# Summing two scan units by four products of 64 rows and 64 columns, and without folding quads by DMA

## The chip, the core and the metric

The kernel runs on one NeuronCore of a Trainium2 chip. A time is the device time of one execution in microseconds (us); the figure for a kernel is the median of its runs. The core has a matrix engine (TensorE, PE in the profile, with its weight loads as PEld), VectorE (DVE), ScalarE (ACT), GpSimd (POOL), SyncE (SP), which here only starts transfers, and DMA queues.

## The reference, cut to what matters

A batch of 8 sequences of 512 tokens and 256 features goes through four layers: a linear attention (layer 0), two selective state-space layers (1 and 2) and another linear attention (layer 3). The two state-space layers fill nearly the whole time, and the change is in them. Each has 512 channels and 16 states per channel:

```python
def step(h, inp):
    dt_t, B_t, C_t, u_t = inp
    dA = jnp.exp(dt_t[:, :, None] * A)
    h = h * dA + (dt_t * u_t)[:, :, None] * B_t[:, None, :]
    y = jnp.einsum('bdn,bn->bd', h, C_t)      # the sum over the 16 states
    return (h, y)
...
y = jnp.transpose(ys, (1, 0, 2)) + u * D_param
y = y * jax.nn.silu(z)
return jnp.einsum('bsd,ed->bse', y, out_proj_w)
```

## The kernel before, in words

**Tiling.** A scan is one state-space layer of one sequence: 16 in all (`SCANS`). The 512 channels are 4 chunks of 128 partitions, the 512 tokens lie in the free dimension. The chunks are taken in two halves of 2 chunks. A **unit** is one state n of one chunk: a tile of 128 partitions x 512 tokens of float32. Unit g of a half is state n = g // 2 and chunk c2 = g % 2; two units that share a state are a **pair**. So a half has 32 units (16 pairs), a scan 64, the kernel 1024 units or 512 pairs.

**A unit's way.** ScalarE makes the decay `exp(dt * A)` (L1028 in a PSUM bank, L1044 in SBUF). The input dt*u*B is made for a pair at once, by GpSimd (L756, kind BESIDE, 192 pairs) or by VectorE (L1318, kind SPREAD, 320 pairs, from a B row that ScalarE copied into a bank, L1036). VectorE runs the recurrence over the tokens, unit by unit (`scan`, L1325 and L1328). GpSimd multiplies the pair by its row of C (`weight`, L765). TensorE sums over the states (`sum_up`, L1648): the identity times the state tile, added up in one of two PSUM banks, `y_banks[c2]`, one for each chunk. The first product of a bank is `skip` (L1638), the diagonal matrix of D times u. After the last sum VectorE multiplies the bank by silu(z) (`gate`, L1340), and `m_gate` tells TensorE that the bank may be used again. The state tiles stand in a ring of 20 (`STATES`); `state_free` waits until a slot has been summed.

**Folding.** Four units in a row are a quad, 8 quads a half. `FOLDS = ((0, 1), (3, 4))` names two quads a half that are not summed by TensorE but added onto the next one by a DMA that accumulates in SBUF (`fold`, L769, started by GpSimd). TensorE then sums 24 of the 32 units of a half; the units of quads 1 and 4 come late (`FOLDED_LAG` 14 units after their scan, the others `SUM_LAG` 5), and wait for the DMA (`m_fold`).

**Order.** Every engine walks the same clock of units (`run_batches`): at unit g it issues its own part of unit g, and chains of other work (attention of other sequences, the preparation of the next scan, the output of the last one) are laid between the units by hand-written tables of ticks (`ATT_STAGES`, `PREP_STAGES`, `POST_STAGES`, ...; `HALF_STEPS` sets how far ahead ScalarE and GpSimd issue). `sum_ticks` says at which unit which sum is issued (`SUMS_AT`), and `GATE_TICKS` at which unit VectorE gates a bank. Each engine executes its own list strictly in order, so a waiting instruction holds all behind it. On TensorE the sums stand between the products of attention (L1416 to L1494), of the preparation (L1516 to L1555) and of the output (L1602, L1610).

**Numbers to keep in mind.** A float32 product of TensorE is shown by the profile as two records of MATMUL, each with its own LDWEIGHTS. 32 halves x 24 sums are 768 products (1536 records at L1648), and 64 skips are 128 records at L1638.

Of the kernel before, what the change touches and what calls it, by code (L numbers as in the profile page):

```python
# [5 lines left out]
P = 128  # L6
B, T, D = 8, 512, 256
TT, DC = T // P, D // P
DI, CH, N = 512, 4, 16
# [8 lines left out]
HALVES = 2  # L18
# [4 lines left out]
PAIRS = B // 2  # L23
SLOTS = 4

SUM_LAG = 5
BANKS, DECAYS, STATES, ROWS = 3, 7, 20, 4
QUAD = 4
FOLDS = ((0, 1), (3, 4))
FOLD_LAG = 2  # L30
# [216 lines left out]
def sum_ticks():  # L247

    at = {}
    for g in range(ALL_UNITS):  # L250
        if not fold_from(g):
            at.setdefault(g + (FOLDED_LAG if fold_into(g) else SUM_LAG), []).append(g)
    return at
# [3 lines left out]
SUM_ORDER = [g for tick in sorted(SUMS_AT) for g in SUMS_AT[tick]]  # L257
SUM_COUNT = {g: n for n, g in enumerate(SUM_ORDER, 1)}
BANK_SUMS = {}
for unit_ in SUM_ORDER:  # L260
    BANK_SUMS.setdefault((unit_ // HALF_UNITS, unit_ % HC), []).append(unit_)
GATE_TICKS = tuple(max(t for t, units in SUMS_AT.items() for k in units if k < HALF_UNITS and k % HC == c2) + 1 - HALF_UNITS
                   for c2 in range(HC))

# [156 lines left out]
def bass_cond_seq(nc, x, out, mask_cols, keep_cols, mask_rows0, mask_rows3, order, const_pack, att_packs, ssm_packs,  # L421
# [4 lines left out]
    with ctx:  # L426
# [634 lines left out]
        def _(dve):  # L1061
# [268 lines left out]

            def gate(si, half, c2):

                layer, s = scan_of(si)
                c = half * HC + c2
                if c == 0:
                    taken(dve, prep_fill(si, "z2"))
                    taken(dve, prep_fill(si, "z3"))
                dve.wait_ge(m_sum, SUM_COUNT[BANK_SUMS[si * HALVES + half, c2][-1]])
                taken(dve, prep_fill(si, f"z{c}"))
                dve.tensor_tensor(u[s][:, c, :], y_banks[c2][:], zh[s][:, c, :], ALU.mult).then_inc(m_gate, 1)  # L1340

            def unit(g, part):
                if part == 0:
                    for first in (g, g + 1):
                        if is_unit(first) and first % HC == 0 and kind_of(first) == SPREAD and PRODUCT_LEAD[first // HC] == first - g:
                            inject(first)
                    return
                if is_unit(g):
                    scan(g)
                for c2, tick in enumerate(GATE_TICKS):  # L1350
                    if g % HALF_UNITS == tick and is_unit(g - HALF_UNITS):
                        si, half, *_ = split(g - HALF_UNITS)
                        gate(si, half, c2)

# [4 lines left out]
        def _(pe):  # L1359
# [268 lines left out]

            def skip(si, half, c2):
                layer, s = scan_of(si)  # L1630
                c = half * HC + c2
                if c < HC:
                    pe.wait_ge(s_gate_nat, 2)
                    pe.wait_ge(s_mod[3], 1)
                    pe.wait_ge(s_skip, 2)
                past(pe, m_gate, si * CH + c - HC + 1)
                pe.wait_ge(p_u, si * CH + c + 1)
                pe.matmul(y_banks[c2][:], skip_diag[layer][:, c, :], u[s][:, c, :], start=True, stop=False)  # L1638

            def sum_up(g):  # L1640
                si, half, n, c2, c = split(g)
                in_bank = BANK_SUMS[g // HALF_UNITS, c2]
                if g == in_bank[0]:
                    skip(si, half, c2)
                pe.wait_ge(m_prod, g // HC + 1)
                for n in fold_into(g):
                    pe.wait_ge(m_fold[n], 16 * (g // HALF_UNITS) + 16)
                pe.matmul(y_banks[c2][:], ident, state[:, g % STATES], start=False, stop=(g == in_bank[-1])).then_inc(m_sum, 1)  # L1648

# [91 lines left out]
```

## Time and profile before

| | |
|---|---|
| median of 3 runs | 2156.11 us (2149.99 to 2160.99) |
| span of the profiled execution | 2153.9 us |
| VectorE busy | 1935.2 us, 90% |
| TensorE busy | 1887.8 us, 88% |
| GpSimd busy | 1821.9 us, 85% |
| ScalarE busy | 1719.8 us, 80% |
| mean granted TensorE clock | 0.968 of full speed |

The median lies 2.2 us over the span of the one profiled execution. Busy shares are means over the span. The first 200 us (set-up, two attentions of sequences 0 and 1, the first preparation) and the last 110 us (output and a lone attention) look different from the 1800 us between, in which the scans run back to back.

### The profile page before, as it was taken

The numbers are of one execution on the slowest core, as the hardware profiler recorded it, in microseconds if no ns is written. First come the engines' busy times: TensorE is split into PE (matmuls) and PEld (weight loads), VectorE is DVE, ScalarE is ACT, GpSimd is POOL, SyncE is SP. The second block draws the span as 40 slices with busy tenths as digits, with TensorE's granted clock in tenths as the row PEclk, the third lists the DMA queues.
The fourth block names the chain that finished last, engine by engine and source line by source line (L and its number), as shares of the span: only waits on it lengthen the run. The fifth ranks groups of instructions, "written<-read, shape, count | busy, mean of one in ns | idle before, by whom it ended". The sixth has DMA issues, their size and how long they took to land. (4 is left out here: it accounts for less than half of the span.)

```text
span 2153.9 us, 22717 instructions
## 1 busy us (share of the span) xinstructions
PE 1887.8 (88%) x5980; PEld 975.5 (45%) x5980; DVE 1935.2 (90%) x2022; ACT 1719.8 (80%) x3125; POOL 1821.9 (85%) x906
## 2 busy tenths in 40 slices
PE   8968789899888989899898989899899988778798
PEld 7533334445354544445454443535445443324356
DVE  5479999999999999999999998999999999899963
ACT  2387788888889888898989888888989987677652
POOL 0088998989898998989899997989989898989950
PEclk9889989999999999999999999999999999899999
DMA  6056665656466575646656675555556666555630
GB/s 247 1 170 174 176 195 150 196 168 185 138 178 176 165 207 166 196 146 180 173 160 187 176 209 155 167 176 164 171 165 195 173 181 179 174 166 176 192 93 20
DMA packets 170543, 358.77 MB, mean 167 GB/s; under 512 B 19544, under 2 KB 27952, under 8 KB 161712
## 3 DMA queue, kind: packets, MB, share of 16 engines
q1 hardware_dynamic: 151958, 279.32, 39.8%
q0 software_dynamic: 9216, 67.11, 15.3%
q10 hardware_dynamic: 9242, 10.89, 1.5%
q8 instruction: 49, 0.80, 0.1%
q14 instruction: 78, 0.64, 0.1%
HBM read 284.85 MB, written 5.29 MB: 135 GB/s over the span
## 5 line engine op out<-in xcount | busy, mean ns | idle before, releaser
L765 POOL TENSOR_TENSOR state<-state,c_rows 128x1024 f32<-128x1024 f32 x512 | 1214.9, 2410 | 139.2 <-DVE state L1328 95.8
L1648 PE MATMUL bank<-state,const_sb 128*128 128x512 f32 x1536 | 775.3, 620 | 111.2 <-POOL state L765 63.7
L1328 DVE TENSOR_TENSOR_SCAN state<-decay,mix_banks 128x512 f32<-128x512 f32 x640 | 753.2, 1207 | 31.5 <-ACT decay L1044 14.5
L1325 DVE TENSOR_TENSOR_SCAN state<-mix_banks,state 128x512 f32<-128x512 f32 x384 | 450.4, 1204 | 30.5 <-ACT mix_banks L1028 19.7
L1648 PEld LDWEIGHTS bank<-state,const_sb 128*128 128x128 f32 x1536 | 282.2, 196 | 423.9 <-issue 252.3
L756 POOL TENSOR_TENSOR state<-kept,b_rows 128x1024 f32<-128x1024 f32 x192 | 469.1, 2443 | 3.4 <-DMA b_rows<-flat_rows 1.7
L1044 ACT ACTIVATE decay<-kept,ssm_pack 128x512 f32<-128x512 f32 x640 | 435.3, 711 | 1.0
L1318 DVE TENSOR_TENSOR mix_banks<-kept,mix_banks 128x1024 f32<-128x1024 f32 x320 | 392.8, 1227 | 28.9 <-ACT mix_banks L1036 19.6
L1028 ACT ACTIVATE mix_banks<-kept,ssm_pack 128x512 f32<-128x512 f32 x384 | 259.5, 683 | 115.7 <-DVE state L1328 101.2
L1544 PE MATMUL bank<-kept,ssm_pack 128*128 128x512 f32 x512 | 244.2, 613 | 25.9 <-DVE kept L1277 8.4
L1036 ACT ACTIVATE mix_banks<-b_rows 128x512 f32<-128x512 f32 x320 | 187.8, 591 | 51.2 <-DVE state L1328 27.6
L1435 PE MATMUL bank<-att_pack,xnT 128*128 128x256 f32 x704 | 202.1, 405 | 0.0
L1544 PEld LDWEIGHTS bank<-kept,ssm_pack 128*128 128x128 f32 x512 | 96.4, 195 | 146.2 <-issue 105.6
L1602 PE MATMUL bank<-kept 128*128 128x256 f32 x512 | 130.0, 396 | 16.2 <-DVE kept L1291 16.2
L708 POOL TENSOR_TENSOR att_rstd<-att_var_eps,neg_half 128x4 f32<-128x4 f32 x32 | 35.4, 1105 | 120.1 <-DVE att_minus L1165 112.3
L1435 PEld LDWEIGHTS bank<-att_pack,xnT 128*128 128x128 f32 x704 | 119.2, 189 | 37.6 <-issue 8.1
L1277 DVE SCALAR_TENSOR_TENSOR kept<-bank,ssm_pack,kept 128x511 f32<-128x511 f32 (+2 forms) x192 | 128.7, 737 | 7.4 <-ACT kept L974 7.1
L1602 PEld LDWEIGHTS bank<-kept 128*128 128x128 f32 x512 | 99.9, 201 | 47.5 <-issue 35.9
L728 POOL TENSOR_TENSOR kept<-kept 128x1024 f32<-128x1024 f32 x32 | 77.5, 2421 | 48.3 <-ACT kept L942 48.3
L1044 ACT ACT_TABLE_LOAD x82 | 105.2, 1283 | 1.5
L1422 PE MATMUL bank<-xnT,att_pack 128*128 128x512 f32 x120 | 60.1, 624 | 21.7 <-ACT xnT L875 16.0
L1416 PE MATMUL bank<-const_sb,xn 128*128 128x128 f32 x352 | 56.7, 285 | 25.0 <-ACT xnT L929 8.8
(198 smaller groups left out, 2208.7 us busy)
## 6 DMA issues: line engine op xcount, KB each, us to landing
b_rows<-flat_rows SPq DMA_DIRECT2D x512, 256.0 KB, 3.9
c_rows<-flat_rows SPq DMA_DIRECT2D x512, 256.0 KB, 3.6
state<-state POOLq DMA_DIRECT2D x64, 1024.0 KB, 9.7
out<-x_res ACTq DMA_DIRECT2D x8, 512.0 KB, 7.4
ssm_pack<-ssm_pack SPq DMA_DIRECT2D x2, 2035.0 KB, 13.2
x_next<-x ACTq DMA_DIRECT2D x6, 512.0 KB, 7.2
state<-ada_w SPq DMA_DIRECT2D x1, 1536.0 KB, 12.3
kept<-ada_w SPq DMA_DIRECT2D x1, 1536.0 KB, 15.1
```

What stands on the lines that cost most here:

```text
L756: pool.tensor_tensor(pair_states(g), dtu[:, c:c + HC], by_pair(b_rows[:, row % ROWS]), ALU.mult).then_inc(m_inject[BESIDE], 1)
L765: pool.tensor_tensor(st, st, by_pair(c_rows[:, row % ROWS]), ALU.mult).then_inc(m_prod, 1)
L1028: act.activation(mix_banks[BANK_OF[g]], dt[:, c, :], ACT.Exp, scale=neg_a[scan_of(si)[0]][:, c * N + n:c * N + n + 1]).then_inc(m_decay[BE ...
L1036: act.activation(mix_banks[ROW_BANK[g // HC]], b_rows[:, row % ROWS], ACT.Copy).then_inc(m_brow, 1)
L1044: act.activation(decay[:, nth(g) % DECAYS, :], dt[:, c, :], ACT.Exp, scale=neg_a[scan_of(si)[0]][:, c * N + n:c * N + n + 1]).then_inc(m_d ...
L1318: dve.tensor_tensor(both, dtu[:, c:c + HC, :], by_pair(mix_banks[row]), ALU.mult).then_inc(m_inject[SPREAD], 1)
L1325: ins = dve.tensor_tensor_scan(st, mixed, st, 0.0, ALU.mult, ALU.add)
L1328: ins = dve.tensor_tensor_scan(st, decay[:, nth(g) % DECAYS], mixed, 0.0, ALU.mult, ALU.add)
L1435: ins = pe.matmul(dst, lhs[:, c, t * P:(t + 1) * P], weights[:, c, :], start=(c == 0 and bias is None), stop=(c == DC - 1))
L1544: ins = pe.matmul(dst[:], w_in[:, c, (at + e) * P:(at + e + 1) * P], xnT_[:, c, :], start=(c == 0), stop=(c == DC - 1))
L1602: ins = pe.matmul(dst[:, (t % 2) * D:(t % 2 + 1) * D], lhs[:, c, t * P:(t + 1) * P], weights[:, c, :], start=(c == 0), stop=(c == CH - 1))
L1648: pe.matmul(y_banks[c2][:], ident, state[:, g % STATES], start=False, stop=(g == in_bank[-1])).then_inc(m_sum, 1)
```

## The change

The two PSUM banks no longer stand for the two chunks of a half but for the two row halves of a chunk (`ROW_HALVES`, partitions 0 to 63 and 64 to 127). Bank k takes the rows of half k: chunk 0 in its partitions 0 to 63, chunk 1 in 64 to 127. A pair is summed by four products with 64 rows and 64 columns of the identity, one for each combination of row half and chunk; each uses one quarter of the array, and the four use different quarters. Only the last of the four raises `m_sum`, and counts are now per pair. The skip product is cut in the same way. `FOLDS` is empty: no fold transfers, no `m_fold`, and all 16 pairs of a half are summed, each 5 units after its second unit (`SUM_LAG`). `gate` runs for both banks at one unit (`GATE_TICK`), after the last pair of the half, and the first skip of a half waits until both banks of the half before are gated. So that the gated result has its channels in the new order, the columns of `w_in` that make z and the rows of `w_out` are permuted on the host (`by_half`).

```diff
+ROW_HALVES = (slice(0, P // 2), slice(P // 2, P))
-FOLDS = ((0, 1), (3, 4))
+FOLDS = ()
...
-    for g in range(ALL_UNITS):
+    for g in range(0, ALL_UNITS, HC):
         if not fold_from(g):
-            at.setdefault(g + (FOLDED_LAG if fold_into(g) else SUM_LAG), []).append(g)
+            at.setdefault(g + 1 + (FOLDED_LAG if fold_into(g) else SUM_LAG), []).append(g)
...
-                dve.wait_ge(m_sum, SUM_COUNT[BANK_SUMS[si * HALVES + half, c2][-1]])
+                dve.wait_ge(m_sum, SUM_COUNT[HALF_SUMS[si * HALVES + half][-1]])
                 taken(dve, prep_fill(si, f"z{c}"))
-                dve.tensor_tensor(u[s][:, c, :], y_banks[c2][:], zh[s][:, c, :], ALU.mult).then_inc(m_gate, 1)
+                dve.tensor_tensor(u[s][:, c, :], y_banks[k][:], zh[s][:, c, :], ALU.mult).then_inc(m_gate, 1)
...
-                past(pe, m_gate, si * CH + c - HC + 1)
-                pe.wait_ge(p_u, si * CH + c + 1)
-                pe.matmul(y_banks[c2][:], skip_diag[layer][:, c, :], u[s][:, c, :], start=True, stop=False)
+                past(pe, m_gate, si * CH + half * HC)
+                pe.wait_ge(p_u, si * CH + half * HC + HC)
+                for k, rows in enumerate(ROW_HALVES):
+                    for c2, to in enumerate(ROW_HALVES):
+                        c = half * HC + c2
+                        pe.matmul(y_banks[k][to, :], skip_diag[layer][rows, c, rows], u[s][rows, c, :], start=True, stop=False)
...
-                pe.matmul(y_banks[c2][:], ident, state[:, g % STATES], start=False, stop=(g == in_bank[-1])).then_inc(m_sum, 1)
+                for k, rows in enumerate(ROW_HALVES):
+                    for c2, to in enumerate(ROW_HALVES):
+                        ins = pe.matmul(y_banks[k][to, :], ident[rows, rows], state[rows, (g + c2) % STATES],
+                                        start=False, stop=(g == in_half[-1]))
+                ins.then_inc(m_sum, 1)
...
+    by_half = np.arange(DI).reshape(HALVES, HC, 2, P // 2).transpose(0, 2, 1, 3).reshape(DI)
...
+        w_in = np.concatenate([w_in[:, :DI], w_in[:, DI:][:, by_half]], axis=1)
+        w_out = w_out[by_half]
```

What it moves shows in the order of the instructions. The skip line is L1638 before and L1640 now, the sum line L1648 before and L1652 now; one row of the order is one product (not one record), `x4` four in a row. First TensorE, where the second half of the third scan (the first of layer 2) begins: L1533 and L1544 prepare the next scan, L1416, L1422 and L1424 are attention. Before:

```order
242 L1533 MATMUL bank<-permute,kept 128x512 x2
243 L1648 MATMUL bank<-state,const_sb 128x512
244 L1533 MATMUL bank<-permute,kept 128x512 x2
245 L1648 MATMUL bank<-state,const_sb 128x512
246 L1533 MATMUL bank<-permute,kept 128x512
247 L1416 MATMUL bank<-const_sb,xn 128x128 x4
248 L1544 MATMUL bank<-kept,ssm_pack 128x512 x4
249 L1416 MATMUL bank<-const_sb,xn 128x128 x4
250 L1422 MATMUL bank<-xnT,att_pack 128x512 x2
251 L1424 MATMUL bank<-right_rows,bias_rows 128x512
252 L1544 MATMUL bank<-kept,ssm_pack 128x512 x4
253 L1638 MATMUL bank<-kept,skip_diag 128x512
```

And TensorE at the same place now:

```order
241 L1652 MATMUL bank<-state,const_sb 64x512 x4
242 L1533 MATMUL bank<-permute,kept 128x512
243 L1416 MATMUL bank<-const_sb,xn 128x128 x4
244 L1640 MATMUL bank<-kept,skip_diag 64x512 x4
245 L1652 MATMUL bank<-state,const_sb 64x512 x4
246 L1544 MATMUL bank<-kept,ssm_pack 128x512 x4
247 L1652 MATMUL bank<-state,const_sb 64x512 x4
248 L1416 MATMUL bank<-const_sb,xn 128x128 x4
249 L1652 MATMUL bank<-state,const_sb 64x512 x4
250 L1422 MATMUL bank<-xnT,att_pack 128x512 x2
251 L1424 MATMUL bank<-right_rows,bias_rows 128x512
252 L1652 MATMUL bank<-state,const_sb 64x512 x4
```

The skip has moved to the front of the half, and a group of four small products stands between the other work at each pair. Over the whole program there are 544 such groups (512 sums, 32 skips) in 425 places, at 347 of them a single group. Products that use another part of the array than the one before them follow each other 1250 times now and 540 times before.

GpSimd, in the same half, about the second of its two folds; L756 and L765 are the input and the weighting of a pair, L728 part of the preparation. Before:

```order
133 L765 TENSOR_TENSOR state<-state,c_rows 128x1024 x2
134 L728 TENSOR_TENSOR kept<-kept 128x1024
135 L765 TENSOR_TENSOR state<-state,c_rows 128x1024
136 L769 DMA state<-state 128x2048
137 L756 TENSOR_TENSOR state<-kept,b_rows 128x1024
138 L765 TENSOR_TENSOR state<-state,c_rows 128x1024 x3
```

The same place now; only the DMA of the quad has gone:

```order
116 L765 TENSOR_TENSOR state<-state,c_rows 128x1024 x2
117 L728 TENSOR_TENSOR kept<-kept 128x1024
118 L765 TENSOR_TENSOR state<-state,c_rows 128x1024
119 L756 TENSOR_TENSOR state<-kept,b_rows 128x1024
120 L765 TENSOR_TENSOR state<-state,c_rows 128x1024 x3
```

VectorE, at the end of a half, as a piece of the difference (the scan is listed under another name here, and L1340 is the gate):

```order
-L1328 SCALAR_TENSOR_TENSOR state<-decay,mix_banks 128x512 x2
-L1340 TENSOR_TENSOR kept<-bank,kept 128x512
-L1328 SCALAR_TENSOR_TENSOR state<-decay,mix_banks 128x512
-L1340 TENSOR_TENSOR kept<-bank,kept 128x512
+L1328 SCALAR_TENSOR_TENSOR state<-decay,mix_banks 128x512 x3
+L1340 TENSOR_TENSOR kept<-bank,kept 128x512 x2
```

The first of the two gates has moved back by one scan, next to the second.

## Rows read from the trace of the kernel before

**Rows 1.** The page's part 1: busy us (share of the span) xinstructions of each engine.

```profile
PE 1887.8 (88%) x5980; PEld 975.5 (45%) x5980; DVE 1935.2 (90%) x2022; ACT 1719.8 (80%) x3125; POOL 1821.9 (85%) x906
```

**Rows 2.** Busy us of each engine by stretch, then granted clock, DMA share, GB/s.

```profile
core 0: us, PE busy (x) PEld busy (x) DVE busy (x) ACT busy (x) POOL busy (x), PEclk, DMA share, GB/s
0.00:100.00 100.00, 89.44 (x466) 64.89 (x467) 49.80 (x142) 31.80 (x55) 7.02 (x18) 0.90 0.37 134
100.00:200.00 100.00, 71.56 (x202) 33.39 (x202) 81.80 (x80) 81.69 (x147) 80.83 (x40) 0.90 0.53 159
...
600.00:800.00 200.00, 178.73 (x568) 91.64 (x567) 193.96 (x190) 178.47 (x345) 190.74 (x94) 0.99 0.64 187
800.00:1000.00 200.00, 183.28 (x561) 89.35 (x560) 189.70 (x192) 176.73 (x305) 179.80 (x88) 1.00 0.56 165
...
2050.00:2154.00 104.00, 93.24 (x478) 65.04 (x476) 48.49 (x77) 36.09 (x72) 29.80 (x18) 0.99 0.17 50
```

**Rows 3.** Waits of VectorE, 200 to 1900 us: us in total, times, longest.

```profile
DVE mix_banks L1318 <- ACT mix_banks L1036: 18.1, 18, 2.8
DVE state L1328 <- ACT decay L1044: 13.4, 7, 4.7
DVE qstat L1217 <- PE bank L1435: 7.5, 6, 1.3
DVE state L1325 <- ACT mix_banks L1028: 5.5, 9, 1.0
DVE state L1325 <- POOL state L756: 4.7, 9, 1.0
DVE kept L1277 <- ACT kept L974: 4.2, 4, 2.4
DVE x_res L1298 <- PE bank L1602: 4.1, 1, 4.1
```

**Rows 4.** Waits of TensorE in the same stretch, the longest two.

```profile
PE bank L1648 <- POOL state L765: 45.7, 49, 4.0
PE bank L1648 <- DMA state<-state: 43.3, 27, 5.1
```

**Rows 5.** Groups by line and shape: busy us, mean ns, then idle before.

```profile
L1648 PE MATMUL bank<-state,const_sb 128*128 128x512 f32 x1536 | 775.3, 620 | 111.2 <-POOL state L765 63.7 <-DMA state<-state 47.0
L1638 PE MATMUL bank<-kept,skip_diag 128*128 128x512 f32 x128 | 67.8, 612 | 0.0
L1516 PE MATMUL bank<-x_dbl,ssm_pack 64*128 64x512 f32 x128 | 63.5, 616 | 3.1 <-ACT x_dbl L983 3.1
L769 POOL DMA_DIRECT2D state<-state x64 | 55.8, 872 | 0.0
```

**Rows 6.** TensorE's timeline: start us, us, instructions; full-array products in a row.

```profile
1003.32 1.02 PE L1638 MATMUL bank<-kept,skip_diag 128*128 128x512 f32 x2
1004.17 1.02 PE L1648 MATMUL bank<-state,const_sb 128*128 128x512 f32 x2
1005.03 0.59 PE L1602 MATMUL bank<-kept 128*128 128x256 f32 x2
1005.46 1.02 PE L1638 MATMUL bank<-kept,skip_diag 128*128 128x512 f32 x2
```

**Rows 7.** TensorE's timeline where 64-row products (L1516) stand between full ones.

```profile
359.67 1.45 PE L1648 MATMUL bank<-state,const_sb 128*128 128x512 f32 x3
361.05 1.98 PE L1516 MATMUL bank<-x_dbl,ssm_pack 64*128 64x512 f32 x4
362.96 2.41 PE L1648 MATMUL bank<-state,const_sb 128*128 128x512 f32 x5
```

**Rows 8.** The chain that ended last, near its end: start us, us, what.

```profile
1986.45 10.69 DMA state<-state
```

**Rows 9.** Who waited for the gate (L1340), and for whom it waited: us, times.

```profile
  PE bank L1648: 6.3, 6
who waited for it (us, times):
  PEld bank L1602: 17.4, 3
```

More of the change, by code:

```diff
@@ L257 @@
 SUM_ORDER = [g for tick in sorted(SUMS_AT) for g in SUMS_AT[tick]]
[L258 to L263, printed above, removed]
+SUM_COUNT = {g + k: n for n, g in enumerate(SUM_ORDER, 1) for k in range(HC)}
+HALF_SUMS = {}
+for pair_ in SUM_ORDER:
+    HALF_SUMS.setdefault(pair_ // HALF_UNITS, []).append(pair_)
+GATE_TICK = max(t for t, pairs in SUMS_AT.items() for k in pairs if k < HALF_UNITS) + 1 - HALF_UNITS
 def prep_fill(pi, what):
@@ L1329, in scan, with gate @@
                 ins.then_inc(m_scan, 1)
-            def gate(si, half, c2):
+            def gate(si, half, k):
                 layer, s = scan_of(si)
-                c = half * HC + c2
+                c = half * HC + k
                 if c == 0:
@@ L1349, in unit @@
                     scan(g)
[L1350 to L1353, printed above, removed]
+                if g % HALF_UNITS == GATE_TICK and is_unit(g - HALF_UNITS):
+                    si, half, *_ = split(g - HALF_UNITS)
+                    for k in range(HC):
+                        gate(si, half, k)
             run_batches(setup, attention, before, tail, after, unit)
@@ L1627, in after, with skip @@
                 yield from w.to("end")
-            def skip(si, half, c2):
+            def skip(si, half):
                 layer, s = scan_of(si)
-                c = half * HC + c2
-                if c < HC:
+                if half == 0:
                     pe.wait_ge(s_gate_nat, 2)
@@ L1635, in skip @@
                     pe.wait_ge(s_skip, 2)
-                past(pe, m_gate, si * CH + c - HC + 1)
-                pe.wait_ge(p_u, si * CH + c + 1)
-                pe.matmul(y_banks[c2][:], skip_diag[layer][:, c, :], u[s][:, c, :], start=True, stop=False)
+                past(pe, m_gate, si * CH + half * HC)
[4 more added lines that the diff above has]
+                        pe.matmul(y_banks[k][to, :], skip_diag[layer][rows, c, rows], u[s][rows, c, :], start=True, stop=False)
             def sum_up(g):
[L1641 to L1644, printed above, removed]
+                si, half, *_ = split(g)
+                in_half = HALF_SUMS[g // HALF_UNITS]
+                if g == in_half[0]:
+                    skip(si, half)
                 pe.wait_ge(m_prod, g // HC + 1)
```

## The prediction, made before the kernel ran

> **What bounds the kernel now.** I read the page's first part and the busy time by stretch first [rows 1, 2]. VectorE has the largest share, 1935.2 of 2153.9 us, and between 600 and 1000 us, where the scans run back to back, it is busy 194.0 and 189.7 of 200 us. TensorE has 178.7 and 183.3 there and GpSimd 190.7 and 179.8. VectorE's idle time lies at the two ends: 50.2 and 18.2 us in the first two stretches, 55.5 us in the last. Between 200 and 1900 us its seven longest waits add up to 57.5 us [rows 3]: 41.2 for ScalarE, 11.6 for TensorE, 4.7 for GpSimd. So the kernel is bound by VectorE, with GpSimd and TensorE close behind. TensorE's own waits are for its inputs: 45.7 us for GpSimd's weighting and 43.3 us for the fold transfer [rows 4]. It is not the bound, but it has only 266 us to spare over the whole span. Whoever adds more than that makes it the bound.
>
> **What a product costs.** The sums are 1536 records in 775.3 us, the skips 128 in 67.8 us [rows 5]: together 843.1 us. All else on TensorE is 1887.8 - 843.1 = 1044.7 us. In a row of full products the next one starts 0.85 and 0.86 us later [rows 6], so a record takes 0.43 us of the array, and each shown record has a tail of about 0.17 us behind it (1.02 for two records). A product on half the rows is no shorter: L1516 works on 64 rows and shows 616 ns where the sums have 620 and the skips 612 [rows 5]. So each of the four small products takes the two records of 0.43 us of a full one, and the change can win on TensorE only if products in different quarters of the array run at the same time. No row of before shows two products in separate parts of the array side by side; this is the unknown on which all hangs.
>
> **A change of the part in use.** Between 359.67 and 365.37 us stand 3 full records, 4 of 64 rows and 5 full ones [rows 7]: 5.70 us, where 12 x 0.43 + 0.17 = 5.33. The two changes of part cost 0.37 us, some 0.19 each. The order shows 710 more of them: 710 x 0.19 = 135 us. The nearest row is this one for 64 rows; for 64 columns I take the same, with 0.10 (71 us) and 0.25 (178 us) as bounds.
>
> **The sum of TensorE, if four run together.** A group of four takes 2 x 0.43 = 0.86 us: 544 x 0.86 = 468, and the tails in 425 places 425 x 0.17 = 72. With the rest, 1045 + 468 + 72 + 135 = 1720 us, 168 less than now although all 512 pairs are summed. TensorE then has 434 us to spare.
>
> **What goes elsewhere.** GpSimd loses 64 issues of 872 ns, 55.8 us [rows 5], and so leads VectorE by a bit more; TensorE no longer waits 43.3 us for folds. None of this is on VectorE, which keeps each of its instructions. It wins only out of its waits [rows 3]: nearly all of those for TensorE and GpSimd (15 us), and of the 41.2 us for ScalarE a quarter (10 us), because ScalarE is late where attention products, which now stand behind fewer sums, reach it late. Near the end the chain has one fold transfer of 10.69 us [rows 8], but there VectorE was hardly idle, so I give it 2 us; and the last gate of the kernel comes after one group and not two products, 1 us. Together 28 us. The bounds are 0 (the waits only change their names) and 62 (all 57.5, and 5 at the end).
>
> **What the new gate adds.** Both gates now stand after the last pair, and the first skip of a half waits for both; before, the skips came seven units later and waited for nothing. TensorE can be ahead of VectorE by up to two units of some 1.9 us at this place, so it may stand up to 4 us in each of 32 halves, 120 us. If four run together, the 434 us cover this. What is queued behind it is what stands there in the order: preparation products and attention, and ScalarE and VectorE wait for those. VectorE waited 6.3 us for L1648 at the gates until now [rows 9]; I add 4 us, with 0 and 30 as bounds. The host's permutation of weights costs nothing: the same shapes are loaded.
>
> Against the profiled execution: 2153.9 - 28 + 4 = 2130 us of span. The median lies 2.2 us above that span, so the forecast is **2132 us**, with 2095 to 2165 as its own range.
>
> **Rival 1: the products stagger.** The two records of a product use the same quarter, so the second must follow the first. If TensorE starts its records strictly in the order of the program, the first record of the next product can only go with the second of the last one: a group takes five record times and not two, and four more for each group directly behind it. Then 544 x 4 x 0.43 = 936, and 425 x (0.43 + 0.17) = 255 us; 1045 + 936 + 255 + 135 = 2371 us. TensorE is the bound, and its idle time at the ends stays, 39 us in the first two stretches and 11 in the last [rows 2]: 2421 us of span, with waits at the gates some 2430 us. For it speaks that in every row TensorE's records follow each other in the order of the program; against it only that no row shows it with free quarters. It is the rival on the slow side, and it decides as soon as a group costs more than (2154 - 50 - 1045 - 72 - 135) / 544 = 1.57 us: below that TensorE still fits beside VectorE.
>
> The Trainium skill, "TensorE: Matmul & The Clock Gate", Part 3 (Packing small matmuls), says that products in different tiles run concurrently and that matmuls are in program order in start and in end. Read strictly, the second half of this speaks against the change, for a float32 product is two records, and this rule would give rival 1; the figures there are for packs in which each tile gets one record. By the first half alone the sum is the forecast. The same part says that a weight load overlaps a running product only in another row group; taken strictly, even full products could not follow at 0.43 us with their loads, and here the trace differs, so I give these rules no more weight than the rival has.
>
> **Rival 2: half of it runs together.** Only the row halves, or only the column halves, are independent, and the two products that share one follow each other. A group takes six record times, 2.57 us: 544 x 2.57 = 1398, and with the same ends 255; 1045 + 1653 + 135 + 50 = 2883 us.
>
> **Rival 3: nothing runs together**, the change doesn't do what it says. 8 x 0.43 = 3.43 us a group: 1866 + 72 + 1045 + 135 + 50 = 3168 us. For rivals 2 and 3 speaks only that no row shows the contrary.
>
> **Rival 4: four run together, but the gate takes the gain.** At 4 us of TensorE in each half, if a quarter of it comes through to VectorE by the queued attention products, 32 us are added: about 2165 us.
>
> **How the numbers follow.** Four together 0.55 (rival 4 apart), rival 1 0.25, rival 2 0.08, rival 3 0.09, rival 4 0.03. I put the forecast first because nothing in the rows ties a record to one that uses another quarter, and the change of part (0.19 us) shows that the array does treat a part as a part. A measurement of this kernel can tell 0.5%, 11 us, from no change. Of the 0.55, 0.42 is below 2145 us and 0.13 is within 0.5%, since the bounds of VectorE's gain reach to 0; every rival is slower by more than 0.5%, or close to it: faster 0.42, same 0.13, slower 0.45. Both signs hold much, so the range must reach from the forecast's low end over rival 1: 2095 to 2480 us leaves out rivals 2 and 3 and the edges.
>
> **What would show each step.** In the profile after: the starts of a group's eight records (in pairs within 0.43 us: forecast; in steps of 0.43 us over 2.15: rival 1; over 3.4: rival 3); TensorE's busy time, 1585 us without the changes against over 2200; VectorE's busy share in the middle, 96% or, if TensorE bounds, under 88%; the wait of L1640 for the gate L1340. The prediction is wrong as soon as the four do not run together; where they do, it is wrong if the granted clock falls below the 0.99 and 1.00 of the middle stretches because TensorE has less to do, so that the attention products come later than now.

## The result, and the profile after

The changed kernel takes **2262.84 us** (median of 4, 2260.75 to 2265.9), the kernel before 2157.64 us beside it: a ratio of 1.0486, interval 1.0459 to 1.0513. It is slower by 105 us. The forecast was 2132 us.

The page's first part of the kernel after (busy us, share of the span, instructions of each engine):

```profile
PE 1847.3 (82%) x8668; PEld 809.4 (36%) x8668; DVE 1940.5 (86%) x2022; ACT 1720.3 (76%) x3125; POOL 1769.2 (78%) x842
```

Against [rows 1] GpSimd is busy for 52.7 us less and TensorE for 40.5 us less; ScalarE (1719.8, now 1720.3) and VectorE (1935.2, now 1940.5) have the same work, and all of them stand idle for longer. No engine has become the bound in place of VectorE; the loss is waiting. All of VectorE's waits over the whole run add up to 281.6 us, where the kernel before has 181.2: 187.0 for TensorE (before 101.3) and 86.7 for ScalarE (before 64.2). That is 100 of the 105 us.

Four products do run together. TensorE's timeline after, with one group at 1003.95 us:

```profile
1003.42 0.60 PE L1435 MATMUL bank<-att_pack,xnT 128*128 128x256 f32 x2
1003.95 1.09 PE L1652 MATMUL bank<-state,const_sb 64*64 64x512 f32 x8
1004.97 1.99 PE L1544 MATMUL bank<-kept,ssm_pack 128*128 128x512 f32 x4
```

Eight records, four products of 512 columns, lie within 1.09 us, and the next product starts 1.02 us after the start of the group. In narrower windows of the same timeline four of the eight records have started by 1003.99 us, none more by 1004.41, and all by 1004.45. In [rows 6] one full product of two records has 1.02 us, and 0.85 us to the next one. So a group of four costs what one full product costs, plus the two changes of part (0.10 us before the group, 0.16 behind it, and 0.10 in the longer first record of what follows: 0.36, where [rows 7] had 0.37).

Busy us by stretch after, with the granted clock behind the five engines, to be held against [rows 2]:

```profile
core 0: us, PE busy (x) PEld busy (x) DVE busy (x) ACT busy (x) POOL busy (x), PEclk, DMA share, GB/s
600.00:800.00 200.00, 162.77 (x803) 72.58 (x803) 178.19 (x177) 164.57 (x298) 170.36 (x80) 0.92 0.40 133
800.00:1000.00 200.00, 169.98 (x736) 66.53 (x740) 179.98 (x180) 167.62 (x318) 165.77 (x79) 0.88 0.42 137
```

VectorE's share fell from 97 and 95% to 89 and 90%. The clock of TensorE fell from 0.99 and 1.00 to 0.92 and 0.88; it has two levels, 1.2 and 2.4 GHz, so 0.88 means that it stood at the lower one for 24% of the stretch. Over the whole run the mean is 0.893, before it was 0.968.

VectorE's waits between 200 and 1900 us after (us in total, times, longest):

```profile
DVE v L1238 <- PE bank L1494: 41.3, 18, 4.8
DVE mix_banks L1318 <- ACT mix_banks L1036: 21.6, 19, 2.7
DVE kept L1340 <- PE bank L1652: 17.9, 16, 1.9
DVE kept L1277 <- ACT kept L974: 13.5, 9, 2.1
DVE state L1328 <- ACT decay L1044: 10.6, 7, 2.4
DVE att L1227 <- PE bank L1485: 10.3, 6, 3.3
DVE qstat L1217 <- PE bank L1435: 7.6, 10, 1.2
```

Against [rows 3], where VectorE waited 11.6 us for TensorE, it now waits 77.1 us for it in these seven rows, although TensorE has less to do. A wait of 4.8 us for L1494 stands there six times, twice in every four scans (at 520, 648, 1050, 1177, 1579 and 1706 us), and makes 28.8 of the 41.3 us. TensorE's timeline at one such place, 1167 to 1180 us:

```profile
1167.74 0.69 PE L1610 MATMUL bank<-ssm_pack,const_sb 8*128 8x256 f32 x2
1171.60 1.98 PE L1640 MATMUL bank<-kept,skip_diag 64*64 64x512 f32 x8 [3.17 <-DVE kept L1340]
1173.34 1.96 PE L1652 MATMUL bank<-state,const_sb 64*64 64x512 f32 x8
1175.22 2.02 PE L1494 MATMUL bank<-att,kexp 128*128 128x128 f32 x8
```

VectorE's timeline at the same place:

```profile
1170.08 1.26 DVE L1340 TENSOR_TENSOR kept<-bank,kept 128x512 f32<-128x512 f32 x2
1171.26 1.21 DVE L1291 TENSOR_TENSOR kept<-ssm_pack,bank 128x1024 f32<-128x1024 f32 x1
1177.29 0.69 DVE L1238 TENSOR_TENSOR v<-bank,qstat 128x512 f32<-128x512 f32 x1 [4.81 <-PE bank L1494]
```

TensorE stands 3.17 us before the skip (L1640), until VectorE has gated both banks (L1340). Skip and first sum follow, and only then attention's product L1494, for which VectorE then waits. The two groups take 1.98 and 1.96 us, not 1.09: TensorE is at its lower clock for them, and the granted clock between 1167 and 1180 us is 0.74. The group just before TensorE's wait, at 1166.72 us, still takes 1.08 us, and the one at 1179.18 us takes 1.09 us again. So one place shows both suspects: **G**, the early first sums behind the gate, in front of attention; and **C**, the clock that falls where TensorE has less to do.

### The profile page after: what moved, and what is told of

The parts are those of the page before. It is cut to its first block and busy times, and to the rows that moved or that the text cites. A ratio compares the mean times of both kernels' runs of the same rounds, so it can differ in the third digit from the quotient of the medians.

```text
span 2259.1 us, 27725 instructions
## 1 busy us (share of the span) xinstructions
PE 1847.3 (82%) x8668; PEld 809.4 (36%) x8668; DVE 1940.5 (86%) x2022; ACT 1720.3 (76%) x3125; POOL 1769.2 (78%) x842
## 5 line engine op out<-in xcount | busy, mean ns | idle before, releaser
L765 POOL TENSOR_TENSOR state<-state,c_rows 128x1024 f32<-128x1024 f32 x512 | 1199.1, 2357 | 291.8 <-DVE state L1328 182.6
L1652 PE MATMUL bank<-state,const_sb 64*64 64x512 f32 x4096 | 618.6, 682 | 126.2 <-POOL state L765 126.2
L756 POOL TENSOR_TENSOR state<-kept,b_rows 128x1024 f32<-128x1024 f32 x192 | 453.0, 2360 | 0.1
L1652 PEld LDWEIGHTS bank<-state,const_sb 64*64 64x64 f32 x4096 | 121.5, 143 | 400.8 <-POOL state L765 239.2
L1544 PE MATMUL bank<-kept,ssm_pack 128*128 128x512 f32 x512 | 245.6, 610 | 11.3 <-DVE kept L1277 4.4
L1435 PE MATMUL bank<-att_pack,xnT 128*128 128x256 f32 x704 | 209.2, 416 | 0.0
L1544 PEld LDWEIGHTS bank<-kept,ssm_pack 128*128 128x128 f32 x512 | 89.6, 190 | 156.5 <-issue 118.8
L1435 PEld LDWEIGHTS bank<-att_pack,xnT 128*128 128x128 f32 x704 | 121.2, 194 | 43.5 <-issue 14.3
L1416 PE MATMUL bank<-const_sb,xn 128*128 128x128 f32 x352 | 67.0, 322 | 74.8 <-ACT xn L836 31.1
L1602 PEld LDWEIGHTS bank<-kept 128*128 128x128 f32 x512 | 91.6, 192 | 67.8 <-issue 58.7
L728 POOL TENSOR_TENSOR kept<-kept 128x1024 f32<-128x1024 f32 x32 | 75.3, 2353 | 45.6 <-ACT kept L942 45.6
L1416 PEld LDWEIGHTS bank<-const_sb,xn 128*128 128x128 f32 x352 | 46.2, 162 | 132.8 <-ACT xn L836 43.1
```

The source lines that it names most:

```text
L756: pool.tensor_tensor(pair_states(g), dtu[:, c:c + HC], by_pair(b_rows[:, row % ROWS]), ALU.mult).then_inc(m_inject[BESIDE], 1)
L765: pool.tensor_tensor(st, st, by_pair(c_rows[:, row % ROWS]), ALU.mult).then_inc(m_prod, 1)
L1435: ins = pe.matmul(dst, lhs[:, c, t * P:(t + 1) * P], weights[:, c, :], start=(c == 0 and bias is None), stop=(c == DC - 1))
L1544: ins = pe.matmul(dst[:], w_in[:, c, (at + e) * P:(at + e + 1) * P], xnT_[:, c, :], start=(c == 0), stop=(c == DC - 1))
L1602: ins = pe.matmul(dst[:, (t % 2) * D:(t % 2 + 1) * D], lhs[:, c, t * P:(t + 1) * P], weights[:, c, :], start=(c == 0), stop=(c == CH - 1))
L1652: ins = pe.matmul(y_banks[k][to, :], ident[rows, rows], state[rows, (g + c2) % STATES], start=False, stop=(g == in_half[-1]))
```

## The experiments

Each time stands beside runs of the kernel before on the same chip; ratios are to those. Line numbers differ by a few where lines were added.

### Undoing one part each

**Folds kept.** The one edit to the changed kernel:

```diff
-FOLDS = ()
+FOLDS = ((0, 1), (3, 4))
```

> The changed kernel with one part undone: FOLDS is ((0, 1), (3, 4)) again, so TensorE sums 12 of the 16 pairs of a half by groups of four small products, quads 0 and 3 are folded by DMA, and the first skip of a half comes after the first unfolded pair, seven units later than now. Theory G (the first skip right behind the gate holds TensorE, and attention's products behind it): the wait of L1640 for L1340 (36.6 us) goes, VectorE's 41 us for L1494 go, time near 2160 to 2190. Theory C (TensorE has less to do, is granted its lower clock level more often, and everything on the way through it is later): TensorE has even less to do, mean clock below 0.89, time 2250 or more.

Measured: 2209.99 us, ratio 1.0246 (1.021 to 1.0282), clock 0.882. Half the loss is gone, and VectorE's waits for L1494 fell from 41.3 to 2.2 us. The clock is as low as C said, but the time hit neither number: more than G alone was left.

**Full products without folds**, the kernel before with `FOLDS = ()`.

> The kernel before with the folds taken off alone: full 128 x 128 products, 32 sums a half, 1024 in all. It adds 256 products of 0.86 us, 220 us, to TensorE, whose spare time was 266 us, and its first skips also come right behind the gates. Theory C expects a mean clock of 0.97 or more, since TensorE is nearly always at work, and a time of 2230 to 2300 because TensorE is then the bound. Theory G expects the L1494 wait of VectorE here as well. If it is slower than the changed kernel, the four products side by side are worth the difference.

Measured: 2377.15 us, 1.1019 (1.0982 to 1.1057), clock 0.952, TensorE 90% busy. Without folds the changed kernel, with its small products and its order by pairs, is 114 us faster than this. So the small products do win where TensorE has too much to do; the gain is used up by what taking off the folds costs. The run was slower than the 2230 to 2300 us of C, and its clock lower than C's 0.97. VectorE's wait for L1494 is there, as G said (42.5 us, and 48.2 us for L1435 beside it).

**First sums late**, the changed kernel with another `sum_ticks`:

```diff
-            at.setdefault(g + 1 + (FOLDED_LAG if fold_into(g) else SUM_LAG), []).append(g)
+        tick = max(first + 11, g + 1 + SUM_LAG)
+        while len(at.get(tick, [])) == 2:
+            tick += 1
+        at.setdefault(tick, []).append(g)
```

> The changed kernel with the sums of the first pairs of each half issued late: pairs 0 and 1 at unit 11 of the half, 2 and 3 at 12, the rest as they were. The skip goes with them, and has the gate well behind it. No instruction is added or taken away. Theory G: the wait of L1640 for L1340 goes to nearly 0 and so does most of VectorE's wait for L1494, 60 to 100 us are won back, time 2160 to 2200. Theory C: the clock stays near 0.89 and the time falls by less than 20 us, to 2245 or more.

Measured: 2215.71 us, 1.0269 (1.0228 to 1.031), clock 0.897. Only the places of the first four sums and the skip in a half have changed, with no work added or taken away, and 47 us are won back. TensorE's wait for the gate at the skip (line 1643 here) is gone: the trace lists 12.7 us of idle time before it, all of it "issue". VectorE's waits, 200 to 1900 us, the line for v now 1241 and for attention's product 1497:

```profile
DVE kept L1343 <- PE bank L1655: 20.3, 15, 1.9
DVE mix_banks L1321 <- ACT mix_banks L1039: 20.0, 22, 1.6
DVE state L1331 <- ACT decay L1047: 19.5, 5, 8.9
DVE state L1328 <- ACT mix_banks L1031: 14.8, 15, 2.4
DVE v L1241 <- PE bank L1497: 11.6, 6, 3.3
```

41.3 us have become 11.6. G is shown, with a size of 47 us (60 to 100 had been expected); C's expectation (less than 20) is missed. The 47 us are those of the places and the wait for the gate together, at this kernel's clock; how much of them the lower clock makes is not separated. And 59 us over the kernel before are left.

**More work on TensorE**: a second group with a zero block of the identity before every other group.

```diff
+                if g // HC % 2:
+                    for k, rows in enumerate(ROW_HALVES):
+                        for c2, to in enumerate(ROW_HALVES):
+                            pe.matmul(y_banks[k][to, :], ident[rows, ROW_HALVES[1 - k]], state[rows, (g + c2) % STATES],
+                                      start=False, stop=False)
```

> The changed kernel with a second group of four small products before every other group, on the same state tiles but with a block of the identity that is zero, so that it adds 0 to the sums: 256 more groups of 0.86 us, 220 us more work for TensorE, in the same order otherwise. Theory C: the mean clock rises from 0.89 to 0.95 or more, and the time stays at 2263 or falls, to 2200 to 2260, though there is more to do. Theory G: the added work stands in front of attention's products as well, time 2290 to 2380.

Measured: 2307.03 us, 1.0694 (1.0655 to 1.0733), clock 0.944. The clock rose nearly as far as C said; the time rose by 44 us for some 220 us of added work (TensorE's busy time rose by 148). That misses C's 2200 to 2260 us and lies in G's range. Since the added groups also push other products back, the run does not say what the clock alone is worth.

### Form of the product against place in the order

**Full products by pair**: e1's kernel with two full products for each pair in place of the four small ones.

```diff
-                for k, rows in enumerate(ROW_HALVES):
-                    for c2, to in enumerate(ROW_HALVES):
-                        ins = pe.matmul(y_banks[k][to, :], ident[rows, rows], state[rows, (g + c2) % STATES],
-                                        start=False, stop=(g == in_half[-1]))
+                for c2 in range(HC):
+                    ins = pe.matmul(y_banks[c2][:], ident, state[:, (g + c2) % STATES], start=False, stop=(g == in_half[-1]))
```

> The kernel of e1_folds_kept with the form of the product alone put back: a pair is summed by two full products instead of four small ones, in the same place of the order, with the same folds, the same gates next to each other and the counts by pair. Against e1 (2210 us) it has 12 x 32 x 0.86 = 330 us more on TensorE. Theory C (the clock that follows from less work costs the time): mean clock back at 0.96 or more and the time back near 2154, 2145 to 2170. Theory O (order by pairs, the gates together and the tables of ticks that were fitted to the old order cost it): it stays at 2200 or more, with the clock back all the same.

Measured: 2190.09 us, 1.0142 (1.0112 to 1.0172), clock 0.951. Both theories take a part: with the work and nearly the clock of before it is still 33 us slower than before (the order by pairs), and e1, with 330 us less on TensorE at 0.86 us a product (186 us less of busy time in the profile), is 20 us slower than this.

**Work put before the wait**: e3's kernel with a zero group of 256 columns before each pair's wait, from the fifth scan on.

```diff
+                if g >= 4 * UNITS:
+                    for k, rows in enumerate(ROW_HALVES):
+                        for c2, to in enumerate(ROW_HALVES):
+                            pe.matmul(y_banks[k][to, 0:256], ident[rows, ROW_HALVES[1 - k]], permute[rows, 0, 0:256],
+                                      start=False, stop=False)
```

> The kernel of e3_first_sums_late with four small products of 256 columns, which add 0, put before TensorE's wait for each pair's weighting, from the fifth scan on: 384 times some 0.43 us, 165 us of work that partly falls into idle time. Theory C: the clock rises from 0.897 to 0.94 or more and the time falls from 2216 to 2170 to 2205. Without an effect of the clock on the time it rises by what of the 165 us doesn't fit into idle time, to 2225 to 2290.

Measured: 2271.62 us, 1.0527 (1.0502 to 1.0552), clock 0.924: slower by 56 us. C's numbers are missed, and the time lies where it would without any effect of the clock. Raising the clock by work that stands in the way does not pay.

**The gate one unit later**, e3's kernel with `+ 2` for `+ 1` in `GATE_TICK`.

> The kernel of e3_first_sums_late with both gates one unit later on VectorE. VectorE's wait of 20 us for L1652 at the gates should go (theory G, second part: the gates stand right behind the last sum) and the time fall by 10 to 20 us, to 2195 to 2206; if the last sum is late only because TensorE is at its lower clock, something else takes the wait and the time changes by less than 8 us.

Measured: 2230.72 us, 1.0333 (1.0311 to 1.0354). VectorE's wait of 20.3 us at the gates went, as G said, but the time rose by 15 us: VectorE waits in other places instead (24.7 us for L1031, where e3 has 14.8; 8.2 us for L1613, which e3's rows do not have). A later gate is no cure.

**Middle sums later too**, e3's kernel with `tick = max(first + 11, min(g + 1 + 7, first + 36))`.

> The kernel of e3_first_sums_late with the sums in the middle of a half two units later as well (7 units after the second unit of a pair; the last pair of the half stays where it is, since the gate needs it). TensorE's wait for GpSimd's weighting at L1652 should nearly go. Theory G (a sum that waits holds attention's products behind it) expects 10 to 30 us less than 2216; theory C expects no more than 8 us either way, since the same idle time only stands in another place.

Measured: 2226.98 us, 1.0316 (1.0297 to 1.0336), 11 us slower than e3, again against G's expectation. The moved sums come together in front of the gate: the last two pairs are now summed in one unit, and VectorE's wait for the last sum grew from 20.3 to 52.6 us. Later is not better as such.

### The clock against the changes of part

**One full product a pair**: e8's kernel with 320 of its 768 sums left out.

```diff
+                    if c2 == g // HC % HC or g in (in_half[0], in_half[-1]):
                         ins = pe.matmul(y_banks[c2][:], ident, state[:, (g + c2) % STATES], start=False, stop=(g == in_half[-1]))
```

> The kernel of e8_full_products_by_pair with half of its sums left out: all but the first and last pair of a half are summed by one full product, of one of their two units, so the result lacks the other unit. TensorE's work for a pair is then 0.86 us, as that of a group of four small products, but without any change of the part of the array in use. Theory C (less work, lower clock, later products): clock 0.88 to 0.90 and a time near that of e1, 2205 to 2215. Theory S (what the small products cost over full ones are the 433 more changes between parts of the array, some 0.19 us each, 82 us of TensorE's time that stand in front of other products): time at or below e8, 2170 to 2192.

Measured: 2210.19 us, 1.0229 (1.0196 to 1.0262), clock 0.895. Less work in the same order, and 20 us slower than e8. That is the time of e1 (2209.99), which has 433 changes of part more. So less work alone can cost what the small products cost, and the changes of part add nothing that shows beside it. The two kernels do not wait in the same places (VectorE's wait for the last sum is 28.1 us here and 15.5 in e1), so the equal times don't prove that the changes are free.

**Two pairs at a time**, e3's kernel with 278 changes fewer: both groups of a quad are issued back to back.

```diff
+        first, second = g // HALF_UNITS * HALF_UNITS, g // QUAD * QUAD + HC
+        at.setdefault(max(first + (11 if g < first + QUAD else 13), second + 1 + SUM_LAG), []).append(g)
...
-                for j in SUMS_AT.get(g, ())[part::2]:
+                for j in SUMS_AT.get(g, ()) if part == 0 else ():
```

> The kernel of e3_first_sums_late with the groups of two pairs issued back to back, behind the later of them: the same products, but 907 changes of the part of the array in use where e3 has 1185. Theory S: 278 x 0.19 = 53 us less on TensorE, time 2185 to 2205. Theory C: idle stretches of TensorE get longer, the clock stays at 0.897 or falls, time 2216 or more.

Measured: 2231.03 us, 1.0333 (1.0303 to 1.0363), clock 0.887. Fewer changes, and 15 us slower, so saving changes does not win here. But the edit moves sums as well: the last two pairs are summed in one unit, and VectorE's wait for the last sum grew from 20.3 to 40.2 us. This run therefore says less on the changes of part than e11.

**The kernel before with cut sums.**

```diff
-                pe.matmul(y_banks[c2][:], ident, state[:, g % STATES], start=False, stop=(g == in_bank[-1])).then_inc(m_sum, 1)
+                cut = slice(0, T // 8 if g // HC % 2 and g not in (in_bank[0], in_bank[-1]) else T)
+                pe.matmul(y_banks[c2][:, cut], ident, state[:, g % STATES, cut], start=False, stop=(g == in_bank[-1])).then_inc(m_sum, 1)
```

> The kernel before, with 320 of its 768 sums cut to 64 of their 512 columns (the result lacks the rest): 320 x 0.75 = 240 us less work for TensorE, no instruction added, taken away or moved. Where every duration stays as it is, less work in the same order can't make anything later: 2157 or a little less. Theory C: the mean clock falls from 0.97 to 0.90 to 0.93 and the time rises to 2168 to 2190 though there is less to do.

Measured: 2192.96 us, 1.0163 (1.0138 to 1.0188), clock 0.902. This is the clearest run of the study. The order, the instructions and the waits are those of the kernel before, except that 320 of the sums leave out seven eighths of their columns; 240 us of work are gone, and the time rises by 36 us. The engines work through their lists in order, so shorter work alone could make nothing later; some other durations must have grown. The first part of its page, with the columns of the one above:

```profile
PE 1799.9 (82%) x5980; PEld 1002.2 (46%) x5980; DVE 1939.3 (88%) x2022; ACT 1719.7 (78%) x3125; POOL 1823.0 (83%) x906
```

Busy us by stretch of the same kernel, with the granted clock behind the five engines:

```profile
600.00:800.00 200.00, 164.91 (x569) 94.32 (x568) 186.92 (x184) 173.16 (x322) 187.10 (x93) 0.92 0.61 177
800.00:1000.00 200.00, 172.01 (x503) 88.25 (x502) 183.83 (x184) 172.02 (x311) 173.10 (x85) 0.91 0.58 168
```

Its group of attention's projections (L1435; busy us, mean ns of one), whose mean was 405 ns in the kernel before:

```profile
L1435 PE MATMUL bank<-att_pack,xnT 128*128 128x256 f32 x704 | 227.1, 445 | 0.0
```

VectorE, ScalarE and GpSimd are busy for the same time as before, within 4.1 us, and the fold transfers land in 9.6 us, before in 9.7. TensorE's busy time fell by only 88 of the 240 us, since most of its products are longer at 0.91 and 0.92 of the clock than at 0.99 and 1.00 [rows 2]: the uncut sums have a mean of 688 ns, before 620. What grew is TensorE's, and it grew with the lower clock. It reaches VectorE, whose waits for TensorE over the whole run are 132.2 us, before 101.3: 31 of the 36 us.

### What the order cost

**One unit earlier**, with small products (e1's kernel, `SUM_LAG = 4`), then with full ones (e8's), then without folds (e3's).

> The kernel of e1_folds_kept with sums and gates one unit earlier (SUM_LAG 4): a pair is summed 4 units after its second unit, which is where the kernel before summed the first unit of a pair. Theory O (the place of the sums and gates in the order): a change of more than 8 us from 2210 one way or the other, down to 2190 if the later gate was the cost of e8 over the kernel before. Theory C: within 8 us.

Measured: 2194.21 us, 1.0165 (1.0128 to 1.0202), 16 us faster than e1: the place matters, as O said.

> The kernel of e8_full_products_by_pair with sums and gates one unit earlier (SUM_LAG 4). If the 33 us of e8 over the kernel before are the later place of sums and gates, 2155 to 2175; if they are the gates standing together or the counting by pairs, 2180 or more.

Measured: 2190.63 us, 1.0155 (1.0125 to 1.0186), the same as e8. This speaks against lateness as such: the first units of the pairs that take in no fold stand where the kernel before has them, the second ones a unit earlier, and nothing is won.

> The kernel of e3_first_sums_late (small products, no folds, first sums late) with SUM_LAG 4. If the same 16 us are won as from e1 to e12, 2195 to 2205, the best form without folds; still slower than the kernel before, since its clock stays near 0.90. Below 2150 would beat both kernels.

Measured: 2268.29 us, 1.051 (1.049 to 1.0531), clock 0.883, 53 us slower than e3, where 2195 to 2205 us were expected. The same edit gives -16, 0 and +53 us. In the last one the sums stand in front of their input, and TensorE waits 147.2 us for GpSimd's weighting at the sums (line 1655), where in e3 it was 65.5 and in [rows 4] 45.7; VectorE in turn waits 37.0 us for attention's product behind them, where in e3 it was 6.8. TensorE's waits of this run, 200 to 1900 us (total, times, longest):

```profile
PE bank L1655 <- POOL state L768: 147.2, 100, 6.0
```

VectorE's waits in the same stretch:

```profile
DVE qstat L1220 <- PE bank L1438: 37.0, 12, 5.9
```

**The gates alone**, the kernel before with both gates at the later unit, and then **the sums too**:

```diff
+GATE_TICKS = (max(GATE_TICKS),) * HC
```

```diff
-            at.setdefault(g + (FOLDED_LAG if fold_into(g) else SUM_LAG), []).append(g)
+            at.setdefault(g // HC * HC + 1 + (FOLDED_LAG if fold_into(g) else SUM_LAG), []).append(g)
```

> The kernel before with one row of VectorE's order changed: the gate of the first chunk stands one unit later, next to that of the second, as in the changed kernel. If e8's 33 us over the kernel before come from the gates, 2180 to 2195; if they come from the sums being issued by pairs, within 8 us of 2157.

> The kernel before with the sum of the first unit of each pair one unit later, in the same tick as that of the second, and so both gates together as well, but with the old counts by unit and a skip for each bank. If the place of the sums and gates is what cost e8 its 33 us, 2180 to 2195; if it is the coupling of the two units (one count for both, both skips first), below 2172.

Measured: the gates alone 2156.17 us, 0.9986 (0.9966 to 1.0007), no difference. With the first unit of each pair summed one unit later: 2183.82 us, 1.0124 (1.0087 to 1.0161), clock 0.957. The edit also moves most of the second units, to the later half of the same unit. So 27 of e8's 33 us come from where the sums stand on TensorE, with no change of form or count; the rest, 6 us, is within what two such medians can differ by. With e14 it can't be lateness alone: what e8, e14 and e18 share is that the two sums of a pair stand in the same unit, and that the first units of the pairs that take in a fold come a unit later. Which of the two is the cause was not tried.

### The account

In steps from the kernel before (2157) to the changed one (2263), each a difference of two medians. The intervals of the ratios reach 6 to 9 us to either side, and the kernel before itself has medians from 2154 to 2160 us beside the different runs, so a step of 6 us is hardly told from nothing. Of the steps only e1 to e3 was measured side by side, and there the runs do not overlap.

| step | us | by |
|---|---|---|
| the two sums of a pair in one unit, the first of them one unit later | +27 | e18 |
| one count a pair, both skips first | +6, within noise | e8 |
| small products: less work, lower clock | +20 | e1; e11 gives the same without them |
| folds off, the first sums of a half still late | +6 | e3 |
| first sums early, in front of attention and behind the gate | +47 | changed kernel against e3 |

The steps add up to the whole because each starts where the last one ended; that is no proof of their sizes, and in another order they would be others. With folds the small products cost 20 us (e8 to e1), without folds the changed kernel is 114 us faster than e2. What each step did to VectorE is read from all its waits over the whole run, in us:

| kernel | span | for TensorE | for ScalarE | all waits |
|---|---|---|---|---|
| before | 2153.9 | 101.3 | 64.2 | 181.2 |
| e15, before with cut sums | 2191.9 | 132.2 | 70.2 | 214.5 |
| e18 | 2180.2 | 123.5 | 64.8 | 203.5 |
| e8 | 2190.4 | 132.9 | 68.0 | 214.2 |
| e1 | 2205.8 | 128.9 | 87.3 | 230.3 |
| e3 | 2216.5 | 151.4 | 82.5 | 241.7 |
| changed | 2259.1 | 187.0 | 86.7 | 281.6 |

Span less waits is 1973 to 1978 us in every row: all that was lost is VectorE waiting, most of it for TensorE. From e8 to e1 it is ScalarE that VectorE waits longer for, by 19 us, though ScalarE's own busy time is the same (1722.6 and 1721.1 us). What stays open: which product is hit in each step, and how much of the steps of place (+27, +47) is made by the lower clock. The tables that place the other work were fitted to the kernel before, and steps of one unit give anything from -16 to +53 us; no rule for the sign came out of the runs. No variant beat the kernel before.

## Why the prediction was wrong, point by point

- **What bounds the kernel** was right: VectorE does, before and after, with its work unchanged.
- **What a product costs, and whether four run together** was the unknown, and it was right: 1.09 us for eight records. Rivals 1 to 3 fall. Four records start together and the other four some 0.45 us behind them. The two records of a full product follow each other at 0.43 us [rows 6], so the first four must be one of each product, although the program names the products one after the other. The Trainium skill, "TensorE: Matmul & The Clock Gate", Part 3 (Packing small matmuls), says that matmuls are in program order in start and end; for float32 products, which are two records each, this trace does not agree. The half on concurrency holds.
- **A change of part** was right in size (0.36 us for two, forecast 0.38); e11 against e1 shows no cost of it in the time.
- **The sum of TensorE** was too low: 1720 us was forecast, 1585 without the changes of part, and the profile has 1847.3. Its tails and records were priced at the higher clock. L1652 alone has 618.6 us, where 540 were forecast with the skips (another 46.5 us at L1640), and the products that the change does not touch have 1182.2 us, where 1044.7 were carried over.
- **What goes elsewhere** is the step that failed. Of its gain of 28 us, 15 were VectorE's waits for TensorE and GpSimd, nearly all of which were to vanish because TensorE has less to do, and 10 a quarter of those for ScalarE. In place of that, VectorE's waits for TensorE grew from 11.6 to 77.1 us in the rows of 200 to 1900 us, from 101.3 to 187.0 us over the whole run, and those for ScalarE from 64.2 to 86.7. The prediction's last sentence named a falling clock as what would make it wrong, but no rival and no price stood for it; e15 puts 36 us on it in the order of before, and e8 against e11 20 us in that of the pairs.
- **What the new gate adds** had the mechanism, attention's products queued behind a skip that waits for the gate, and a size of 4 us with 30 as bound. It measured 47 us (e3). This was rival 4 (four run together, but the gate takes the gain), which had a chance of 0.03 and 32 us. 4 us in each half had been seen as TensorE's idle time, which its spare time covers; but VectorE was the one who paid, 4.8 us at once, where an attention product was next in line.
- **The range** of 2095 to 2480 us holds the measured 2263 by luck: it was stretched over rival 1, which did not happen, while the forecast's own bounds were 2095 to 2165.
- **What wasn't priced at all**: that the sums of a pair's two units move into one unit (+27 us, e18). The prediction looked at how much work stands on TensorE, not at where it stands among the products that others wait for.
- Folds off: GpSimd's 55.8 us less were about right as a sum (52.7). VectorE's waits for GpSimd, 10.8 us over the whole run, fell to 2.8, and more than that VectorE did not have from it.

## What to carry to other kernels

Where one engine bounds and the others are close behind, taking work off one of them need not win anything; ask which of its products the bounding engine waits for, and whether the change puts anything in front of those. In an order that was fitted by hand a sum moved by one place can cost more than the work that is saved, so change the form of an operation and its place in separate steps. Less work for TensorE can also mean longer products: read the granted clock before and after, and price the products that others wait for at the lower level.

## What the runs showed of the hardware that was not expected

- Four float32 products on four quarters of the array run side by side, both records of each: 1.09 us for 8 records of 512 columns, where a full product of 2 records has 1.02. Four of the records start together, the other four some 0.45 us later.
- Cutting 240 us of TensorE's work out of the kernel before made it 36 us slower (ratio 1.0163, 1.0138 to 1.0188), with the mean granted clock down from 0.968 to 0.902 and no other engine's busy time changed by more than 4.1 us; a second pair of kernels, e8 and e11, shows the same with 20 us (clock 0.951 and 0.895).
- Adding work raised the clock (0.893 to 0.944 in e5, 0.897 to 0.924 in e6), but there the work stood in front of what others needed, and the time rose by 44 and 56 us.
